# A two-part layer with attention and gated feed-forward on one core: how much side work goes into each attention step

## What is computed

```python
x = x + _layernorm(_L0_attn_ref(_layernorm(x), w_q, w_k, w_v, w_o))      # 16 heads of 16 features
x = x + _layernorm(_L0_ffn_ref(_layernorm(x), W_r, W_k, W_v, mu_r, mu_k))

# attention
scores = jnp.einsum('bqhd,bkhd->bhqk', q, k) * scale
weights = jax.nn.softmax(scores, axis=-1)
out = jnp.einsum('bhqk,bkhd->bqhd', weights, v)          # then @ w_o.T

# feed-forward; x_prev is x shifted by one token
xr = mu_r * x + (1.0 - mu_r) * x_prev
xk = mu_k * x + (1.0 - mu_k) * x_prev
r = jax.nn.sigmoid(xr @ W_r.T)
k_act = jnp.square(jax.nn.relu(xk @ W_k.T))
out = r * (k_act @ W_v.T)
```

## Time and profile before

| | |
|---|---|
| median of 3 runs | 1409.96 us (1407.97 to 1410.85) |
| time of the profiled execution | 1410.39 us, its span 1408.6 us |
| main loop (first to last values) | 58.9 to 1341.3 us of the span |
| 13 half-batches of the steady kind, u = 1 to 13 | 142.8 to 1186.4 us |
| after the last step | 67.3 us |
| TensorE, ScalarE, VectorE, GpSimd busy | 94%, 75%, 55%, 21% of the span |

### The profile page before, as it was taken

The page is one execution under the profiler, slowest core; times in us unless marked ns, Lnnn a source line. Parts: engine busy times, 40 slices in busy tenths (PEclk is TensorE's granted clock), DMA queues, the critical chain, the costliest instruction groups (busy, mean ns, idle before and its releaser), DMA issues.

```text
span 1408.6 us, 25940 instructions
## 1 busy us (share of the span) xinstructions
PE 1317.9 (94%) x10900; PEld 695.0 (49%) x10900; DVE 779.6 (55%) x1707; ACT 1050.1 (75%) x1143; POOL 292.6 (21%) x366
## 2 busy tenths in 40 slices
PE   4899999999999999999999999999999999999944
PEld 3644455455545455455545545454545554454434
DVE  5162565647475665746475575746576373634454
ACT  1268887888878887888878887787878888887811
POOL 7100122122111321222121221112121112211110
PEclk9599999999999999999999999999999999999956
DMA  3554183305541174304542165203641165000000
GB/s 115 150 137 120 46 165 77 91 16 116 110 107 46 46 155 102 91 16 103 109 106 61 46 136 108 79 26 96 129 91 47 46 133 98 27 1 31 1 16 15
DMA packets 61328, 113.06 MB, mean 80 GB/s; under 512 B 6400, under 2 KB 31232, under 8 KB 61184
## 3 DMA queue, kind: packets, MB, share of 16 engines
q1 hardware_dynamic: 61184, 111.05, 33.2%
HBM read 69.08 MB, written 41.94 MB: 79 GB/s over the span
## 4 chain that ended last, share of the span: by engine, by line
PE 80%; DVE 10%; ACT 4%; POOL 3%; issue 1%; DMA 0%; POOLq 0%
PE O L513 30%; PE S L494 21%; PE M L281 17%; PE M L268 12%; ACT PT L501 4%; DVE A L581 2%; POOL cT L547 1%; DVE sth L572 1%; POOL rsh L577 1%; DVE A L716 1%; DVE CC L537 1%; DVE T L533 1%; DVE T L544 1%; PE M L291 1%; DVE xA L338 1%
## 5 line engine op out<-in xcount | busy, mean ns | idle before, releaser
L501 ACT ACTIVATE PT<-S 128x1024 f32<-128x1024 f32 x1024 | 989.0, 1024 | 234.4 <-PE S L494 233.7
L513 PE MATMUL O<-PT,V 128*17 128x512 f32 x4096 | 542.7, 602 | 0.8
L494 PEld LDWEIGHTS S<-QS,KS 50*128 50x128 f32 x2048 | 175.5, 185 | 473.3 <-ACT PT L501 421.4
L494 PE MATMUL S<-QS,KS 50*128 50x512 f32 x2048 | 394.6, 454 | 15.4 <-ACT PT L501 10.2
L268 PE MATMUL M<-xnT,WH 64*128 64x512 f32 x512 | 132.0, 409 | 10.1 <-DVE xnT L350 10.1
L576 POOL TENSOR_SCALAR veh<-mvh 128x2 f32<-128x2 f32 x96 | 22.6, 235 | 549.4 <-DVE mvh L574 549.4
L513 PEld LDWEIGHTS O<-PT,V 128*17 128x17 f32 x4096 | 68.1, 95 | 106.7 <-issue 55.8
L716 DVE SCALAR_TENSOR_TENSOR A<-Z,M 128x512 f32<-128x512 f32 x30 | 20.6, 688 | 150.9 <-ACT PT L501 131.0
L281 PE MATMUL M<-WH,cT 64*128 64x256 f32 x512 | 88.3, 292 | 13.4 <-DVE cT L547 8.0
L281 PE MATMUL M<-WH,xnT 64*128 64x256 f32 x512 | 98.3, 290 | 1.0 <-DVE WL L775 1.0
L268 PE MATMUL M<-xnT,WL 64*128 64x512 f32 x256 | 96.4, 407 | 0.0
(11 more groups left out here) (104 smaller groups left out, 1692.1 us busy)
## 6 DMA issues: line engine op xcount, KB each, us to landing
scr<-p SPq DMA_DIRECT2D x124, 256.0 KB
QS<-scr SPq DMA_DIRECT2D x60, 256.0 KB, 5.3
KS<-scr SPq DMA_DIRECT2D x60, 256.0 KB, 7.3
QS<-scr SPq DMA_DIRECT2D x68, 128.0 KB, 4.6
KS<-scr SPq DMA_DIRECT2D x68, 128.0 KB, 7.8
xA<-x_dram SPq DMA_DIRECT2D x16, 512.0 KB, 6.8
xB<-x_dram SPq DMA_DIRECT2D x16, 512.0 KB, 5.5
out_dram<-xB SPq DMA_DIRECT2D x15, 512.0 KB, 3.5
```

Source lines behind the costliest of these rows:

```text
L494: fn = lambda e, p=p, a=a, rows=rows: e.matmul(PS[p][:, a, :], KS[qd][rows, p, kt * 128:kt * 128 + 128], QS[qd][rows, p, hf * 512:hf * 512 ...
L501: e_fn = lambda e, p=p: e.activation(PT[i % 2][:, 2 * p:2 * p + 2, :], PS[p][:, :, :], ACT.Exp, scale=SCALE)
L513: fn = lambda e, j=j: e.matmul(PO[32 * j:32 * j + 17, :], V[b % 2][:, kt, 4 * qd + j, :], PT[i % 2][:, j, :], start=(kt == 0), stop=(kt == 7))
```

## The change

`pump` gets a budget of planned time. `due` grows each step by the planned time of what waits, divided by the steps that are left (at most 1.1), and as much is issued, in whole pairs of matmuls, as brings it back under 0.06. A phase can now end and the next begin anywhere in a step; a new phase begins while at least 0.4 is due, and when a second phase of transposes has begun in one step the budget is dropped. Before, a step got half a phase (or all of a short one), and a second half when more halves waited than steps. The costs of a block change from 2 and 1 (counts of halves) to planned times 1.35 and 0.23. In the first eight steps a fixed budget of up to 1.4 takes the place of the full phases. `run_all` now issues, with one call of `pump`, everything that can begin, before resting pieces go on; before, it issued one phase.

```diff
-        step_now = [0]
+        step_now, due = [0], [0.0]
...
-            def __init__(self, chain, half, ready, done, cost=2):
+            def __init__(self, chain, half, ready, done, cost=1.35):
...
-        def pump(left, age=1):
+        def pump(left, most=1.1, age=1):
 
             for block in waiting:
                 if block.seen is None and block.ready() is not None:
                     block.seen = step_now[0]
-            while True:
-                fresh = not (tile[0] or tile[1])
-                if fresh and not begin(age):
-                    return
-                whole = max(sum(cost for cost, _, _ in tile[a]) for a in range(2))
-                stop = max(took) + whole / 2 - .03 if fresh and whole > .5 else 1e9
-                while (tile[0] or tile[1]) and max(took) < stop:
+            todo = sum(block.cost for block in waiting) + max(sum(op[0] for op in ops) for ops in tile)
+            due[0] = min(due[0] + todo / left, most) if left else 1e9
+            short = False
+            while due[0] > (.06 if tile[0] or tile[1] else .4):
+                if not (tile[0] or tile[1]):
+                    if not begin(age):
+                        return
+                    brief = max(sum(op[0] for op in ops) for ops in tile) < .5
+                    if brief and short and left:
+                        due[0] = 0
+                    short = brief
+                before = max(took)
+                while True:
                     put()
-                need = sum(block.cost for block in waiting) + bool(tile[0] or tile[1])
-                if need < left:
-                    return
-                left = need + 1
+                    if not (tile[0] and tile[1]) or abs(took[0] - took[1]) < .05:
+                        break
+                due[0] -= max(took) - before
 
         def run_all():
 
             while waiting or tile[0] or tile[1] or now[0] or resting:
-                pump(0, 0)
+                pump(0, age=0)
...
-            return Block("ahead", turn_half(lambda t, rows: xA[rows, 4 * g + t, c * 128:c * 128 + 128]), ready, done, 1)
+            return Block("ahead", turn_half(lambda t, rows: xA[rows, 4 * g + t, c * 128:c * 128 + 128]), ready, done, .23)
...
-                         have(("xn2", u, 0), ("xn2", u, 1)), done, 1)
+                         have(("xn2", u, 0), ("xn2", u, 1)), done, .23)
...
-                pump(0 if u == 0 and s < 8 else 31 - s)
+                if u == 0 and s < 8:
+                    pump(1, 1.4)
+                else:
+                    pump(max(31 - s, 1))
```

## The result

The changed kernel takes **1472.91 us** (median of 4, 1465.09 to 1475.41) where the kernel before takes 1409.19 on the same chip: a ratio of 1.0442, with 95% between 1.0397 and 1.0486. The forecast was slower, 1443 us; the direction held and the size did not, 30 us lie beyond it.

What follows compares the result with a forecast made beforehand. TensorE's steps, 1.65 us plus side work, were taken to bound the loop. +4.0 per pair x 6.5 gave +26, the end +8, lighter half-batches -1: 1443 us from 1410, own range 1433 to 1450, 8 in 10 within 1428 to 1450.

Steps and rivals of the forecast that it cites:

- filler: Steady pairs of half-batches: side work adds up to 49.5 us in place of 50.0 per 64 steps, -0.5.
- short steps: Steady pairs: 15 steps with under 0.70 us of side work in place of 6, +1.3 us per 64 steps.
- waits for inputs: Steady pairs: TensorE waits about 3.1 us for late inputs at k0, y0, y1 and r1, +1.2 per pair, bounds -1.4 and +3.
- first and two lighter half-batches: Outside the steady loop: 0 for work spread thinner, bounds -3 and +2, and -1 us for the clock staying up.
- end: After the last values: three terms, together +8 us, bounds +4 and +12.
- A step takes 1.65 + F: Loop: a step takes 1.65 us plus its side work F; below F = 0.70 it saves nothing.
- Phase changes inside a step: Steady pairs: a matmul waits for the one just issued, 13 x 0.22 = +2.9 us per pair, bounds 0 and 4.6.
- the waits are covered: Rival, loop and end: waits between matmuls cost half, y0's wait stays as before; about 1425 us, chance 0.16.
- The clock: Rival, y0 and the end: longer TensorE waits bring one or two more low-clock stretches, 3 or 6 us, 1449; chance 0.08.
- Term (1): End: v1 of half-batch 14 has two phases left, not one, so its norm starts later; 3.3 us taken.
- Terms (2) and (3): End: k0 and k1 no longer share phases, 2.7 us; last phases of r1 and v run alone, 2.2 us.
- Faster: Rival, loop: even filling removes the losses if phase changes and input waits cost under 1.5 us per pair; 1400 us, chance 0.05.

Runs made afterwards that it cites:

- e3: Changed kernel with eight throwaway matmuls of 512 columns ahead of k0 in each odd half-batch: 1466.04 us, 1.0387 of the kernel before.
- e2: Changed kernel with y0 and k0 of half-batches 1 to 12 held back one step more: 1427.97 us, 1.0135 of the kernel before.
- e7: e2 with phases beginning only as a step's first side work and a budget limit of 1.4: 1455.54 us, 1.0338 of the kernel before.
- e4: Kernel before with one wait for the matmul just issued added in every long phase: 1445.59 us, ratio 1.0258.
- e5: Kernel before with GpSimd writing the second half of xk's low part four times, so k0's input is late: 1492.28 us, ratio 1.0602.
- e1: Changed kernel with the planner of before in the end (`run_all`) alone, loop untouched: 1467.64 us, 1.0415 of the kernel before.
- e9: Kernel before with one half of a long phase a step, steps ending behind a second transposes phase, next input's norm at steps 23 and 26: 1380.80 us.
- e10: e9 with xk's low part on VectorE in place of GpSimd: 1376.71 us, 0.9782 of the kernel before.
- e12: Changed kernel with steps ending behind the second of two short phases, so transposes spread: 1442.40 us, 1.0218 of the kernel before.
- e11: Changed kernel with the next input's second-half norm moved from steps 13 and 16 to 23 and 26: 1455.34 us, 1.0312 of the kernel before.
- e6: Changed kernel with xk's low part on VectorE in place of GpSimd: 1456.91 us, 1.0350 of the kernel before.

## Why the prediction was right and wrong

The loop and the end, by the forecast's own terms (us):

| term | forecast | measured |
|---|---|---|
| 13 steady half-batches: filler, short steps, phase changes | +18 | +18.1 (what is left) |
| the same: waits for inputs | +8 | +20.0 |
| the same: low clock | 0 | +22.7 |
| first and two lighter half-batches | -1 | -6.4 |
| end | +8 | +6.6 |

The measured column comes from the tables by stretch and the view of waits. Steady part: 1043.7 before, 1104.5 in the changed kernel, 60.8 more. Its half-batches without a low stretch take 84.0 (odd, as 482.60:566.60 above) and 82.6 (even, from e3, where the clock stayed up in half-batches 4 and 8), which makes 1081.8 for the 13 with the first at 83.5 (e3) and the last at 82.7; the rest, 22.7, is clock. Of the 38.1 at full clock, 20.0 are waits for inputs, and 18.1 are left. e2 is 17.4 above the kernel before, but that the two agree is chance: e2 has none of the waits of before, more filler and more short steps. Less 1.1 at the start, the span grew by 60.0.

- **A step takes 1.65 + F, and a short one loses what it is short of 0.70.** Held, as far as e7 can tell: 10.8 lost in all for 12.2 short.
- **Phase changes inside a step, 0.22 each.** Held: 0.20 in phases of 256 columns, fully exposed, and 0.33 where 256 and 512 meet (e4). In the changed kernel the half a = 1 waits for a matmul of its own step in 15 places of a pair, 2 of them there before: the 13 of the forecast. Its rows have 0.33 to 0.34 us from start to start there with 256 columns, 0.44 with 512, so 0.21 is exposed either way. The rival "the waits are covered" falls with it. That the trace decides over an estimate from the Trainium skill's latency ("TensorE: Matmul & The Clock Gate", "Single matmul latency": 0.15 exposed, by estimate) was right. The page's latency itself agrees with the trace, 0.27 us by its formula for 256 columns and 0.28 in e4's rows; what the estimate left out is the 0.06 us from the end of the awaited matmul to the start of the waiting one.
- **Their sum.** +2.8 per pair forecast without the waits for inputs, +2.8 left over in the changed kernel (18.1 / 6.5). Only the sum is shown, and the 0.9 that the forecast took off for overlaps has no row behind it; e2, with 18 short steps and 20 changes, pays 4.1.
- **Waits for inputs: this is the step that failed first.** "k0 ... about 0.5" was 2.6: I saw that xk passes through VectorE and GpSimd, but looked neither at what stands ahead of xk in VectorE's queue in that very step (L343, L549), nor at how the two engines stretch each other. "y0 of the even half-batch ... 1.8" was 1.17 for T and 0.95 for y0, both for a bank and not for cT. With the waits at 29.5 us where 9.5 were, +1.2 per pair was +3.1 (20.0 / 6.5).
- **The clock: the rival priced too low.** I gave it one or two more stretches, 3 to 6 us, since a wait of 0.98 in each pair left the clock alone. A wait of 0.98 says nothing of one of 2.6, and having put the waits too low I put the clock too low as well. It was 51 us in the steady part at half clock, 22.7 lost, 0.44 for each (e5: 24.2 for 51.2, 0.47). The Trainium skill ("TensorE: Matmul & The Clock Gate", "HAM oscillation — how this bites in real kernels") counts half the time at the low level as lost; this trace agrees to within an eighth.
- **The range.** It was narrower than the forecast's own bounds: the waits for inputs (-1.4 and +3 per pair) and the end (+4 and +12) together give 1422 to 1459, where 1433 to 1450 is stated. What was measured lies outside of both, as the clock had no bound but one or two stretches.
- **Empty steps gone, L671 ahead of L650 at the end, ScalarE idle longer.** Right; it idles 66 us more, not 30.
- **The end.** +6.6 for +8. Term (1), v1's two phases: 2.6 later at cT (I had 3.3). Terms (2) and (3), k0 and k1 apart and phases alone: 3.3 together by e1 (I had 4.9). The last 0.7 is not accounted for.
- **The lighter half-batches.** Even filling helped them by 4.1 us, where I had 0 and -1: their empty steps and the low stretch of half-batch 15 are gone. The rest, 2.3, is in the first half-batch, whose length varies by as much (81.0 to 85.4 over the profiles) with the clock at its start.
- **Faster.** The rival said 1400 if phase changes and waits cost under 1.5 per pair. That was not so in the changed kernel. e9 and e10 have 4 phase changes in mid-step in place of 19, by another rule, and are faster than this.

Left open: the same wait of 2.6 us is followed by a low stretch in some half-batches and not in others (k0: 1, 3, 7 and 11 of the changed kernel; 1, 5 and 7 of e1, whose loop has the same instructions). So the program alone does not decide it, and the runs do not say what does. By this the times of single stretches vary between executions, and the 22.7 us are those of the profiled one. The even half-batches' y0 wait was removed only by changes that shift other phases too (e2, e12), so its own price is known from the view of waits alone.

## What to carry to other kernels

When side work is dealt out to fill the gaps of a main loop, price a new schedule by where each block now meets the engines that prepare its inputs and empty its banks, one queue at a time. Here the budget's own steps and phase changes cost 18 us, and that TensorE stood still for inputs and banks cost 43, clock included. The added waits cost 1.6 (e5) to 2.1 times (the changed kernel) their length, since the clock falls behind them. And an even schedule can be worth having once it is kept clear of those meetings: with half a long phase a step, the transposes spread and the norm moved it gave 1.9%, and 2.2% with xk on VectorE as well.

## What the runs showed of the hardware

- A stretch at 1.2 GHz came with single TensorE waits of 2.6 us in 4 of 6 cases (changed kernel) and 3 of 6 (e1), with those of 2.35 to 4.17 us in 13 of 13 (e5), and never with those of 1.31 to 1.33 (7, e11) or 1.70 (6, e6). Two waits in one step, 1.17 and 0.95 us, had one in 6 of 6 (changed kernel, e6), 5 of 6 (e1, e11) or 4 of 6 (e3). With throwaway matmuls through 2.1 us of a wait of 2.6, it stayed at 2.4 GHz (6 of 6, e3).
- A matmul that waits by semaphore for the one just issued starts 0.06 to 0.08 us after its end: 0.33 to 0.35 us after its start with 256 columns and 0.45 with 512, where matmuls without such a wait start 0.12 and 0.235 apart (e4).
- VectorE and GpSimd stretch each other: in the changed kernel L640 took 0.75 us in 23 cases without GpSimd's large operations and 1.65 to 1.67 in 9 beside them, the cast of cT 0.43 alone and 0.99 to 1.46 beside them, and GpSimd's L552 1.27 to 1.68. The Trainium skill ("GPSIMD Engine Reference", "8. Key points") says that the two share their SBUF interfaces and that VectorE instructions with two SBUF inputs contend; the rows agree for L640.
